# A mixture-of-experts tile loop: four tile loads issued at once, batch 6's dispatches put on marks, the late table five places sooner

## The reference

```python
x = x + attention(layernorm(x))          # 16 heads of width 8, causal softmax, projection
x = x + moe(layernorm(x))
# moe, on all 4096 tokens:
top_vals, top_idx = top_k(x @ Wg, 2)     # 8 experts, two for each token
gate = softmax(top_vals);  comb = gate * alpha[expert]
out += comb * (gelu(layernorm_e(x) @ fc1[e] + b1) @ fc2[e] + b2)    # 128 -> 512 -> 128
```

## Time and profile before

| | before |
|---|---|
| runs | 538.74 us median of 3 (537.61 to 540.77) |
| the profiled execution | 539.17 us, span 537.4 us |
| PE busy | 475.5 us, 88% of the span |
| DVE / ACT / POOL busy | 361.2 / 328.2 / 331.4 us |
| granted TensorE clock, mean | 0.971 of full speed |
| chain that ended last | PE 64%, DVE 9%, issue 8%, DMA 6%, POOL 5%, SP's queue 3% |

### The profile page before, as it was taken

How to read it: one execution, slowest core, us unless ns; L and a number is a source line. 1 busy time by engine, 2 the same in 40 slices (tenths; PEclk the granted TensorE clock), 3 DMA queues, 4 the chain that set the end, 5 groups by cost and what they waited for, 6 DMA issues and landing times.

```text
span 537.4 us, 11904 instructions
## 1 busy us (share of the span) xinstructions
PE 475.5 (88%) x3332; PEld 280.8 (52%) x3332; DVE 361.2 (67%) x1284; ACT 328.2 (61%) x694; POOL 331.4 (62%) x691
## 2 busy tenths in 40 slices
PE   3579999999999999999999988787999899999920
PEld 1235444454454454444444443356888678888810
DVE  4597967989889989989988997732457332222226
ACT  2247778687687687687677766663454445555510
POOL 5945735556866866866866866955566456655420
PEclk9989999999999999999999999998999899999975
DMA  2333134134234134234224203177854786566349
GB/s 64 90 85 86 57 102 120 46 105 131 65 108 135 65 105 137 64 106 133 69 87 132 70 27 100 54 217 225 287 159 146 224 268 227 195 199 195 108 163 313
DMA packets 52728, 70.84 MB, mean 132 GB/s; under 512 B 11063, under 2 KB 38430, under 8 KB 52662
## 3 DMA queue, kind: packets, MB, share of 16 engines
q1 hardware_dynamic: 47478, 59.19, 36.4%
q0 software_dynamic: 4320, 8.53, 4.5%
q10 hardware_dynamic: 864, 2.36, 1.2%
HBM read 36.49 MB, written 20.94 MB: 107 GB/s over the span
## 4 chain that ended last, share of the span: by engine, by line
PE 64%; DVE 9%; issue 8%; DMA 6%; POOL 5%; SPq 3%; ACT 2%; another core or an unknown queue 1%; ACTq 0%; POOLq 0%; DVEq 0%
PE acc_bank L733 11%; PE slots L701 11%; PE acc_bank L804 9%; PE slots L718 9%; PE slots L795 9%; DVE masked L1008 3%; PE misc L664 3%; PE slots L697 3%; POOL probs L1321 2%; DMA y_in<-y_dram 2%; POOL z_dram L1312 2%; PE misc L644 2%; PE misc L674 1%; PE misc L667 1%; PE slots L812 1%
## 5 line engine op out<-in xcount | busy, mean ns | idle before, releaser
L876 ACT ACTIVATE probs<-slots 128x512 f32<-128x512 f32 (+1 forms) x352 | 182.2, 564 | 50.3 <-PE slots L718 43.0
L1321 POOL TENSOR_SCALAR_AFFINE_SELECT probs<-probs 128x128 f32<-128x128 f32 (+2 forms) x352 | 117.3, 349 | 72.3 <-ACT probs L876 67.5
L1008 DVE CUSTOM_DVE_ANT_0 masked<-slots,causal_row 128x512 bf16<-128x512 f32 (+1 forms) x256 | 147.0, 616 | 13.6 <-PE slots L701 13.4
L701 PE MATMUL slots<-stack_k,stack_q 125*128 125x256 bf16 (+3 forms) x512 | 128.8, 307 | 6.7 <-DMA stack_q<-parts 4.9
L718 PE MATMUL slots<-stack_q,stack_k 128*128 128x256 bf16 (+3 forms) x512 | 124.9, 299 | 0.3 <-DVE row_max L1008 0.3
L1360 POOL DMA_INDIRECT y_dram<-y,z_in x71 | 69.9, 985 | 57.7 <-issue 16.6
L906 ACT ACTIVATE hidden<-slots,w_in 128x256 f32<-128x256 f32 (+1 forms) x156 | 62.0, 455 | 70.8 <-PE slots L795 62.2
L733 PE MATMUL acc_bank<-probs,v 128*32 128x512 f32 (+3 forms) x1024 | 95.2, 444 | 3.5 <-POOL probs L1321 3.1
L1312 POOL DMA_INDIRECT z_dram<-z,pos x64 | 64.2, 1003 | 24.3 <-issue 11.5
L701 PEld LDWEIGHTS slots<-stack_k,stack_q 125*128 125x128 bf16 x512 | 48.4, 100 | 56.4 <-DVE row_max L1008 19.5
L804 PE MATMUL acc_bank<-hidden,w_in 128*128 128x256 f32 (+1 forms) x312 | 72.1, 374 | 2.6 <-ACT hidden L906 2.6
(11 more groups left out here) (184 smaller groups left out, 486.2 us busy)
## 6 DMA issues: line engine op xcount, KB each, us to landing
w_in<-in_wpack SPq DMA_DIRECT2D x39, 516.0 KB
o_dram<-oT SPq DMA_DIRECT2D x32, 256.0 KB
stack_k<-parts SPq DMA_DIRECT2D x95, 64.0 KB
stack_q<-parts SPq DMA_DIRECT2D x93, 64.0 KB
z_in<-z_dram SPq DMA_DIRECT2D x32, 132.0 KB
xt<-in_x SPq DMA_DIRECT2D x8, 256.0 KB, 3.8
onT<-o_dram SPq DMA_DIRECT2D x8, 256.0 KB
o_inv<-inv_dram SPq DMA_DIRECT2D x8, 256.0 KB
```

The source lines that it names most:

```text
L701: mm = pe.matmul(cols[:, i, :], q[0:K1, hh, blk * P:blk * P + P], k[0:K1, hh, 0:w], start=len(heads) == 1, stop=True, skip_group_check=True)
L876: act.activation(probs_of(n), columns(n, slot), ACT.Exp, scale=SCALE).then_inc(s_exp, 1)
L1008: dve.tensor_tensor_reduce(out=masked[:, n % MASKED, 0:w], in0=slots[:, slot, 0:w], in1=causal_row[:, T - w:T], scale=1.0, scalar=NEG, op0 ...
L1321: pool.affine_select(out=diag, in_=diag, compare_op=ALU.is_ge, fill=0.0, base=0, pattern=[[0, len(heads)], [1, P]], channel_multiplier=-1) ...
```

## The change

Four things change in the schedule. First, loads 0 to 3 all stand at n = 366, ahead of the stores of groups 30 and 31 and of `o_load` in SP's walk; before, loads 2 and 3 stood behind the stores, with `o_load` between them. Second, batch 6's dispatches: before, two stood without a mark ahead of tile 0 and six at marks from tile 0 on; now all eight stand at marks from tile 1 on, so the last is at tile 4's first mark. Scatters shift behind them by up to five marks until tile 26. Third, the late table and the blank rows stand five places sooner, with small changes between the steps: `t_count` and `pad_rows` at place 26 instead of 31, which for SP means behind `load(12)` instead of behind `load(14)`. Fourth, `r_root` of batch 7 goes from place 13 to 15.

```diff
-EARLIEST, FIRST_LOADS = 2, 366
+EARLIEST, FIRST_LOADS = 4, 366
-BORDER_MOVES, LATE_DISPATCH_FROM = 2, 9
+EARLY_DISPATCH_FROM, LATE_DISPATCH_FROM = 1, 9
...
-            7: {... "r_agg": 13, "r_root": 13,
+            7: {... "r_agg": 13, "r_root": 15,
...
-    LATE_OTHER = {"t_count": 31, "t_span": 32, "t_owner": 34, "t_expert": 35, "t_row": 37, "pad_rows": 31}
+    LATE_OTHER = {"t_count": 26, "t_span": 28, "t_owner": 29, "t_expert": 31, "t_row": 32, "pad_rows": 26}
...
-        waiting = [("dispatch", EARLY_BATCHES, i) for i in range(BORDER_MOVES, 2 * NT)]
+        waiting = [("dispatch", EARLY_BATCHES, i) for i in range(2 * NT)]
         plan, ready = {}, 0
-        for i in range(LARGE):
+        for i in range(EARLY_DISPATCH_FROM, LARGE):
...
-    add(("load", EARLIEST), *placed.pop(-1, []), *(("dispatch", EARLY_BATCHES, i) for i in range(BORDER_MOVES)), *(("load", i) for i in range(EARLIEST + 1, AHEAD)))
+    add(*placed.pop(-1, []))
```

More of the change, by code:

```diff
@@ L188, in build @@
     LATE = {6: {"gate": -1, "r_top": -1, "r_exp": -1, "r_comb": 0, "rank": 0},
-            7: {"o_load": -1, "o_invert": 3, "o_spread": 4, "o_scale": 10, "proj": 12, "r_stats": 13, "r_agg": 13, "r_root": 13,
+            7: {"o_load": -1, "o_invert": 3, "o_spread": 4, "o_scale": 10, "proj": 12, "r_stats": 13, "r_agg": 13, "r_root": 15,
                 "r_z": 16, "zT": 18, "gate": 20, "r_top": 21, "r_exp": 22, "r_copy": 19, "r_comb": 24, "rank": 25}}
     LATE_SMALL = 10
-    LATE_OTHER = {"t_count": 31, "t_span": 32, "t_owner": 34, "t_expert": 35, "t_row": 37, "pad_rows": 31}
+    LATE_OTHER = {"t_count": 26, "t_span": 28, "t_owner": 29, "t_expert": 31, "t_row": 32, "pad_rows": 26}
     def moves():
-        waiting = [("dispatch", EARLY_BATCHES, i) for i in range(BORDER_MOVES, 2 * NT)]
+        waiting = [("dispatch", EARLY_BATCHES, i) for i in range(2 * NT)]
         plan, ready = {}, 0
-        for i in range(LARGE):
+        for i in range(EARLY_DISPATCH_FROM, LARGE):
             if i == LATE_DISPATCH_FROM:
```

## The result

The changed kernel takes 546.19 us (median of 4 runs, 542.09 to 548.64), the kernel before 538.17 us (4 runs, 535.26 to 540.77) beside it. The ratio is 1.0131, with a 95% interval of 1.0095 to 1.0167: slower by 7 us (the two medians alone lie 8.0 apart). The profiled execution has a span of 544.5 us where that of before had 537.4.

A forecast was written before the change was run, and what follows sets the result against it. Bound: PE standing still in the tile loop, mainly at the border and tile 14. Sum: -1.1 border, 0 marks and root, +2.4 blank rows, so +1.3; predicted 540.0 us against the median of 538.74, range 535.0 to 543.0.

The forecast's parts named there:

- The border: Start of the tile loop, tiles 2 and 3: loads 2 and 3 sooner, output chain later; gain 1.1 us.
- The delay of DVE: At the border: DVE free of o_invert at 367.7 instead of 364.35, with y(0) and yT(1) queued behind it.
- The bound of 1.2 us of loss: At the border: loss if ACT's second stoppage, 2.29 us, comes behind DVE's wait instead of under it.
- the cover: At the border: ACT's two stoppages would lie under the wait for yT(1) and cost nothing on top.
- the low clock: At fc2(2), behind a gap of over 3 us on PE: 1.5 us added to its end, giving 372.1.
- The slower rival: Output chain and blank rows both cost, border losing 1.2 us and tile 13 2.8: +4.0, 542.7; chance 0.25.
- mostly fixed steps of a short transfer: At the border: why sums was kept at 5.16 us from issue to reciprocal despite room on the DMA engines.
- Blank rows: Tiles 13 to 15: load 13 behind eight writes of 11.5 us; loss 2.1 to 2.8 us, taken as 2.4.
- the price of yT(9): At turn_y(9): PE waits 1.7 us behind t_count and t_span on DVE, ahead of the longer wait for load 13.
- The fast blank rows: Rival at tiles 13 to 15: eight writes take 8.7 us, gain 2.3 us there, total 535.3; chance 0.20.
- Marks and root: Batch 6's dispatches on marks in tiles 1 to 4 and r_root two places later: no cost on PE, 0.

The follow-up runs named there:

- stores early by ACT: Changed kernel, with the stores of groups 30 and 31 issued by ACT right behind its copies, not by SP: 1.0030, again 1.0049 of before.
- late by ACT: Changed kernel, with the last two stores issued by ACT only behind its scaling of tile 1's rows, at about 357: 1.0130 of before.
- pairs with marks: Kernel before, with blank rows written in pairs, batch 6's dispatches on marks from tile 1 and r_root at 15: 0.9976 of before.
- pairs alone: Kernel before, with the eight blank-row writes cut into pairs at places 31, 34, 37 and 40: 1.0000 of before.

## Why the prediction was wrong

**The border: the failed step.** The sum has "Gain 1.1 us" there, 372.1 against the 373.19 at which fc2(2) ended in the trace of before, and "ACT's two stoppages lie under this wait if they come again at the same instructions." The border gained nothing: turn_y(3) came 1.1 us later in the first pair of profiles and 4.6 us later in the second. By the runs, the loads alone cost 2.1 us on the slower chip, and on a faster one the changed kernel costs 4.0 us more than the table alone.

The delay of DVE was forecast nearly right: `o_invert` at 367.7 instead of 364.35, 3.35 us later; measured 3.7 (368.06) and 4.0 (368.51 and 364.48). The price of that delay was wrong. It was set against a time of PE that ACT's stoppages had made in that one trace (370.26, half speed). They are no part of the kernel: in the second trace of before fc2(2) began at 367.87 and was over at 369.76, the marks alone had no stoppage at tile 2, the table alone had one. Without them there is nothing for the wait to lie under, and nearly all of it is paid. The bound of 1.2 us of loss rested on the same cover and was too narrow; the slowest rival, 542.7, so ended 3.5 us short of the measured time.

With the cover, in the first pair, the border still missed its forecast by 2.2 us: fc2(2) began at 369.81 and not at 368.9, and after the gap the low clock, 1.5 us in the sum, cost 1.7 in fc2(2) and 1.05 in fc1(3) (2.94 and 1.89), of which before had paid 0.2. The sum also takes 1.7 us, the distance to the next product, for the 1.89 of fc2(2) itself, and so counts 0.2 us of gain too much.

**A duration carried over that meant something else.** "From the end of the stores' issue to the issue of `sums` it took 359.19 - 355.96 = 3.2 us, so `sums` goes out at about 362.6." In the kernel before SP issued load 2 and `onT` in these 3.2 us and did not wait for the stores at all; in the changed kernel it waited 5.2 us for them, and `sums` went out at 364.7. The slower rival had named the reason ("four loads of 648 KB now lie on the DMA engines ahead of the stores") and then set it aside because the last load was issued 4 us ahead of `sums`. The comparison that counted was with the stores, which followed it by 0.4 us. In the sum this miss of 2.1 us was made good by luck: from its issue to the reciprocal `sums` took 3.3 us and not 5.16 (3.5 with the loads alone, where the dispatches had stayed, so it is not their room), and DVE was free 0.4 us late instead of 2.1. Of the 5.16 us that the prediction called "mostly fixed steps of a short transfer", 1.8 were not fixed. What the late stores cost is shown all the same: with the stores early by ACT 4 us come back, late by ACT they do not.

**Blank rows: right place, and by the runs the right size.** Forecast +2.4, measured 2.5 and 2.6 us by the runs of the table alone on two chips. The places were right: the wait at tile 13's turn, 4.22 us; the writes 5 us sooner; the price of yT(9) with 1.6 us. In the first profile it is +3.4, since SP read the first end 1.1 us late (402.67), behind a yT(8) that was late, took 0.6 us longer for the eight and was through at 414.79 and not at 413.1; from there to PE's turn it took 5.6 us, 5.7 in the forecast.
The fast blank rows came true on the faster chips, at 1.09 us a write, but not as a gain: PE still waited 0.9 to 2.9 us for load 13's rows, since its turn came 3.5 to 5.5 us after their issue and not 2.7; and the hole at tile 14 whose closing was to be the gain isn't there in the kernel before when the writes are fast. That rival counted a gain and its condition that exclude each other.

**Marks and root: nothing, as forecast** (0.9989, and pairs with marks 0.9976 beside pairs alone at 1.0000: 0.2% at most).

**What stays open.** The two parts alone give 0.39% and 0.46% on the first chip, the whole 1.31%; the intervals just leave that, and on a faster chip the sum closes: with the stores early by ACT the changed kernel keeps 0.49%, and the table alone costs 0.49%. Why PE got load 13's rows 3.5 us after their issue in some traces and 5.5 in others was not tried; it is not the border's delay, since with it there are 3.5 (late stores by ACT) and 4.9 and 5.5 us (the changed kernel), and without it 3.9 and 5.4 (early stores by ACT, two chips). Why ACT's late store took a microsecond longer than SP's is open. What the stoppages of the first chips are was not found.

## What to carry to other kernels

A wait that one trace shows in the kernel before is no cover to count on, least of all one without a named releaser: ask whether a second trace has it, and give the sum without it as well. Before a distance between two issues is carried over, ask what filled it, work of the queue or a wait; when an edit moves loads in front of a short store, price the store with their data, whichever queue issues it. In a hand-made order a wait on one engine is paid by the next stage behind it: for each moved block ask which load or which vector operation it now stands ahead of, and when that one is needed. And a rival must be checked for consistency with the profile of before: the condition that makes a step cheap there also removes what it was to save.

## What was not expected of the hardware

The same kernel took 538.8 us on one chip and 526.3 on another (medians of 31 and 25 runs). In the profiles of the slower chips ACT, DVE and POOL stand still for up to 4.4 us with the releaser given as "remote", at other instructions in each; the eleven profiles of the faster chips have not one such wait. From the first to the last of the eight blank writes SP needed 9.3 to 11.4 us there and 8.1 to 8.7 here. In the traces of one of the faster chips, two kernels ran at a distance constant to 0.1 us for 26 tiles. Fc2(2) at half speed followed gaps of 4.1 to 5.4 us. After shorter gaps the length alone does not tell: behind 2.27 and 2.60 us of waiting for tile 13's rows the turn of tile 14 followed after 3.95 us, at full speed, behind 2.78 and 2.86 after 5.63, and in the first trace of before half speed followed 2.12 us (fc2(14) in 3.44 us).
